# A graph kernel whose VectorE one-hots are made in pieces of three visits instead of six

## The chip, the cores and the metric

The kernel runs on one core of a Trainium2 chip. The time is the device time of one execution in microseconds (us). The kernel before was timed three times; its median is 4103.68 us. A profile is one further execution.

## The reference

The inputs are a table x of 12500 nodes by 128 features, 400000 edges (src, dst), sorted by dst, and small weights. Three times, a layer needs for every node the sum of a table's rows over its incoming edges:

```python
h = jnp.maximum(_layernorm(x, axis=-1), 0.0)
m_j = norm[:, None] * (x_j + x_j * x_i @ W1_w.T + W1_b)
out = jax.ops.segment_sum(m_j, to_, num_segments=n)       # layer 0, then a leaky relu, + x
...
agg = jax.ops.segment_sum(h[src], dst, num_segments=n)    # layers 1 and 2
mean_neigh = agg / jnp.maximum(deg, 1.0)[:, None]
return h @ W_self.T + mean_neigh @ W_neigh.T + b
```

The destinations are crowded: node numbers are drawn as the square of a uniform number, so low nodes have many edges and high nodes few.

## The kernel before, in words

Nodes are cut into 98 tiles of 128. The segment sum is made in two ways. For the low, crowded tiles ("dense", 50 in the first pass, then 56 and 57) a matrix of edge counts, 128 destinations by all 98 x 128 sources, is built in SBUF and TensorE multiplies it with the table kept in SBUF as three bf16 parts: `product` (L1460), 98 matmuls a tile. For the other tiles ("tail") the source rows of 128 edges at a time are gathered from HBM with an indirect DMA of GpSimd (`gather`, L1255) and summed by a matmul with a one-hot of the destinations (`subgroup`, L1373).

There are three passes over the graph. In pass 0 (about 285 to 1880 us) the counts of tile g are built while tile g-1 is multiplied; they are stored and loaded again in passes 1 (to about 3010 us) and 2, which build only 7 further tiles between their products.

A count matrix is built from visits. A visit takes 128 edges of blocks of one or two nodes: `visit` (L1431) is one matmul of a one-hot of the source's low 7 bits (128 columns, `hot_low`) with a one-hot of block and high bits (`hot_key`; 98 columns for a block of one node, 196 for a block of two). ScalarE moves the sums from PSUM to SBUF (L1051). VectorE makes the one-hots, `one_hots(f)`: up to 8 visits (blocks of one) or 6 visits (blocks of two) by one instruction for `hot_low` (L1682: 128 columns a visit, so 128x768 for six) and one for `hot_key` (L1685: 128x1176 for six). There are `HOTS = 3` buffers; before it fills one, VectorE waits for `s_visit`, the visits of three buffers ago, and `s_hot` tells TensorE that the buffer is full.

The tail goes in subgroups of 4 or 5 gathers. A ring holds `RSUBS = 5` of them. `ready` (L1710) makes a subgroup's destination one-hot on VectorE in one instruction (128x512 or 128x640) after `s_tail` has freed its place in the ring; `gather` waits for the same; `subgroup` on TensorE waits for `s_S` (the one-hot) and `s_gather` (the landings).

VectorE also does the element work of the layers, in pieces that are put between the one-hots by fixed tables: `take` (L1755 to L1775) reduces the sums of a tile from PSUM, `settle` (L1784 to L1797), `finish` (L1808, L1809) and `split_tile` (L1819 to L1822) follow. All engines run through orders written out beforehand; nothing is scheduled at run time. The visits per block, `vs`, come from the number of edges expected; a batch has `batches[k][1]` nodes a block (1 or 2). In the crowded front, to about 800 us, batches of one and short buffers are frequent; from 800 us on nearly all buffers have six visits of blocks of two.

Of the kernel before, what the change touches and what calls it, by code (L numbers as in the profile page):

```python
# [18 lines left out]
P = 128  # L19
# [19 lines left out]
HOTS = 3  # L39
# [95 lines left out]
def program(nc, x, src, dst, W1, b1, Ws0, Wn0, c0, Ws1, Wn1, c1, out, n_nodes):  # L135
# [111 lines left out]
    with ExitStack() as ctx:  # L247
# [1293 lines left out]
        def _(dve):  # L1541
# [129 lines left out]
            def one_hots(f):  # L1671

                k, b, m, j, n = hots[f]
                deep, width, visits = deepest[k], batches[k][1] * tiles, m * n
                c = b * deep + j
                at_c = slice(c, c + visits) if m == 1 or n == deep else slice(c, c + (m - 1) * deep + 1, deep)
# [5 lines left out]
                dve.tensor_tensor(hot_low[f % HOTS][:, 0:visits * P].rearrange("p (v f e) -> p v f e", v=visits, e=2),  # L1682
                                  low[:, k % 2, at_c, :].unsqueeze(2).to_broadcast([P, visits, P // 2, 2]),
                                  iota_l.rearrange("p (f e) -> p f e", e=2).unsqueeze(1).to_broadcast([P, visits, P // 2, 2]), ALU.is_equal)
                dve.tensor_tensor(hot_key[f % HOTS][:, 0:visits * width].rearrange("p (v f e) -> p v f e", v=visits, e=2),  # L1685
                                  key[:, k % 2, at_c, :].unsqueeze(2).to_broadcast([P, visits, width // 2, 2]),
                                  iota_k[:, 0:width].rearrange("p (f e) -> p f e", e=2).unsqueeze(1).to_broadcast([P, visits, width // 2, 2]),
                                  ALU.is_equal).then_inc(s_hot, 1)
# [14 lines left out]
            def ready(nth, n):  # L1703
# [211 lines left out]
```

## Time and profile before

| | |
|---|---|
| timed runs | 4092.16, 4103.68, 4107.59 us; median 4103.68 |
| profiled execution | 4083.7 us, span 4082.0 us, mean granted TensorE clock 0.989 |
| busy share of the span | TensorE 90%, GpSimd 70%, VectorE 49%, ScalarE 29% |
| chain that ended last | TensorE 40%, GpSimd 36%, issue 12%, VectorE 7%, DMA 4% |
| costliest groups | L1460 3054.3 us (15974 matmuls), L1255 2683.6 us (2643 gathers), L1431 1034.8 us (5102) |
| VectorE one-hots | L1682 881 instructions 475.6 us, L1685 881, 555.9 us, L1710 577, 261.0 us |

Matmuls are pipelined, so a TensorE near 100% is not at its peak. GpSimd's busy time is that of generating its indirect DMAs' descriptors; between two gathers stands a gap of 0.30 us, shown as issue time. An average over the whole span hides that the three passes have different limits.

### The profile page before, as it was taken

To read this page: it belongs to the slowest core of one execution; us is meant where nothing else is said; L and a number is where in the kernel's file an instruction comes from. 1 tells how busy PE (TensorE), PEld (TensorE's weight loads), DVE (VectorE), ACT (ScalarE), POOL (GpSimd) and SP (SyncE) were. 2 spreads that over 40 slices of the span, in tenths; PEclk is the share of its full clock that TensorE was granted. 3 is DMA by queue.
4 is the path that set the end of the run, shared out by engine and by line. 5 is a ranking of instruction groups with operands and counts; after the bars stand their busy time and mean duration, and the time that the engine had idled before them with its cause. 6 is when DMAs were issued, how large, how long until landed. Compare 5 with 4: busy or idle time off the path is not lost.

```text
span 4082.0 us, 67151 instructions
## 1 busy us (share of the span) xinstructions
PE 3657.9 (90%) x24852; PEld 2338.9 (57%) x24852; DVE 2011.0 (49%) x5255; ACT 1180.2 (29%) x3014; POOL 2848.1 (70%) x2859
## 2 busy tenths in 40 slices
PE   0028999999999999998999999999999999999998
PEld 0015666666666666665666665556555656666555
DVE  3579999977777777772233233232321113121211
ACT  0043466666666666661022021121200001000000
POOL 5603877777777777754777777777747777777775
PEclk9998999999999999999999999999999999999999
DMA  5171466666666666558776776766787776777775
GB/s 158 46 181 65 160 216 194 205 208 218 203 220 197 221 200 217 197 190 272 255 252 216 294 252 222 280 238 236 268 277 257 284 253 232 275 273 270 274 267 207
DMA packets 384251, 913.33 MB, mean 224 GB/s; under 512 B 74159, under 2 KB 318088, under 8 KB 363186
## 3 DMA queue, kind: packets, MB, share of 16 engines
q1 hardware_dynamic: 194385, 603.47, 40.0%
q0 software_dynamic: 132000, 274.23, 22.3%
q10 hardware_dynamic: 57536, 31.25, 2.8%
q8 instruction: 205, 3.36, 0.3%
q14 instruction: 125, 1.02, 0.1%
HBM read 664.23 MB, written 245.39 MB: 223 GB/s over the span
## 4 chain that ended last, share of the span: by engine, by line
PE 40%; POOL 36%; issue 12%; DVE 7%; DMA 4%; ACT 1%; DVEq 0%; POOLq 0%; ACTq 0%; SPq 0%
POOL arena L1255 33%; PE ps L1460 30%; PE ps L1373 5%; PE ps L1431 3%; DMA arena<-parts,arena 3%; DVE arena L1685 2%; DVE arena L1682 2%; POOL arena L1220 2%; PE ps L1408 2%; DMA arena<-in_dst 1%; DMA table<-arena 1%; PE ps L1398 0%; ACT arena L1130 0%; POOL arena L1245 0%; POOL arena L1230 0%
## 5 line engine op out<-in xcount | busy, mean ns | idle before, releaser
L1255 POOL DMA_INDIRECT arena<-parts,arena x2643 | 2683.6, 1015 | 950.1 <-issue 790.5
L1460 PE MATMUL ps<-arena 128*128 128x384 bf16 (+1 forms) x15974 | 3054.3, 327 | 19.1 <-DVEq L1759 11.2
L1460 PEld LDWEIGHTS ps<-arena 128*128 128x128 bf16 x15974 | 1544.1, 98 | 931.9 <-ACT arena L1051 21.8
L1051 ACT ACTIVATE arena<-ps 128x392 bf16<-128x392 f32 x1824 | 903.0, 497 | 1007.5 <-PE ps L1431 994.5
L1431 PE MATMUL ps<-arena 128*128 128x196 bf16 (+1 forms) x5102 | 1034.8, 238 | 103.4 <-DVE arena L1685 96.0
L1710 DVE TENSOR_TENSOR arena<-arena 128x640 bf16<-128x640 bf16 (+1 forms) x577 | 261.0, 462 | 1188.0 <-PE ps L1373 1186.9
L1431 PEld LDWEIGHTS ps<-arena 128*128 128x128 bf16 x5102 | 479.2, 101 | 321.4 <-DVE arena L1685 96.9
L1682 DVE TENSOR_TENSOR arena<-arena 128x768 bf16<-128x768 bf16 (+3 forms) x881 | 475.6, 540 | 247.3 <-PE ps L1431 242.6
L1373 PE MATMUL ps<-arena 128*128 128x384 bf16 (+1 forms) x2643 | 532.7, 330 | 63.2 <-DMA arena<-parts,arena 62.8
L1685 DVE TENSOR_TENSOR arena<-arena 128x1176 bf16<-128x1176 bf16 (+4 forms) x881 | 555.9, 631 | 0.0
L1373 PEld LDWEIGHTS ps<-arena 128*128 128x128 bf16 x2643 | 254.4, 98 | 228.0 <-issue 76.3
L1758 DVE TENSOR_REDUCE arena<-ps 128x128 f32<-128x384 f32 x294 | 163.0, 554 | 301.3 <-PE ps L1460 294.7
L1109 ACT ACTIVATE arena<-ps 128x128 f32<-128x128 f32 x196 | 54.1, 276 | 589.3 <-PE ps L1398 589.2
L1408 PE MATMUL ps<-w_t,arena 128*128 128x256 f32 x392 | 120.2, 389 | 20.7 <-issue 17.5
L1220 POOL DMA_INDIRECT arena<-in_dst,arena x98 | 98.0, 1000 | 55.5 <-issue 29.8
L1062 ACT ACTIVATE arena<-ps 128x128 bf16<-128x128 f32 x196 | 54.1, 276 | 281.7 <-DMA table<-arena 218.7
L1245 POOL DMA_INDIRECT arena<-records,first_edge x38 | 47.3, 1246 | 99.4 <-PE ps L1342 79.9
L1408 PEld LDWEIGHTS ps<-w_t,arena 128*128 128x128 f32 x392 | 61.1, 194 | 30.3 <-issue 23.6
L1063 ACT ACTIVATE arena<-ps 128x256 f32<-128x256 f32 x196 | 75.6, 386 | 0.0
L1819 DVE TENSOR_TENSOR arena<-arena,bias 128x128 f32<-128x128 f32 x196 | 56.1, 286 | 33.0 <-ACT arena L1063 32.6
L1323 PE MATMUL ps<-ident,arena 128*63 128x128 f32 x1 | 0.5, 475 | 71.5 <-DVE arena L1600 71.5
L1822 DVE TENSOR_TENSOR arena<-arena 128x128 bf16<-128x128 f32 x196 | 57.4, 293 | 6.8
(155 smaller groups left out, 1177.3 us busy)
## 6 DMA issues: line engine op xcount, KB each, us to landing
arena<-counts SPq DMA_DIRECT2D x102, 3136.0 KB
counts<-arena SPq DMA_DIRECT2D x56, 3136.0 KB
arena<-parts,arena POOLq DMA_INDIRECT x2643
arena<-parts SPq DMA_DIRECT2D x28, 672.0 KB, 9.6
arena<-table SPq DMA_DIRECT2D x196, 64.0 KB
parts<-arena ACTq DMA_DIRECT2D x109, 96.0 KB
parts<-arena SPq DMA_DIRECT2D x14, 679.0 KB, 7.1
parts<-arena SPq DMA_DIRECT2D x87, 96.0 KB
```

Source lines behind the costliest of these rows:

```text
L1051: act.activation(stage[k][:, :, a - g * P:b - g * P], ps[:, unit_bank(q), 0:(b - a) * tiles].rearrange("p (n a) -> p a n", n=b - a), ACT.C ...
L1063: act.activation(yS[:, n % 3, :], bank(7, 0, 2 * P), ACT.Copy).then_inc(s_yS, 1)
L1220: pool.indirect_dma_start(near[q % 7][:, t % HALF, :], None, dst.rearrange("(c e) -> c e", e=P), bass.IndirectOffsetOnAxis(ap=near_i[:, t: ...
L1255: pool.indirect_dma_start(ring[:, m % RSUBS * CHUNKS + c, 0:W0 if nth == 0 else W1C], None, parts_of[nth], bass.IndirectOffsetOnAxis(ap=ta ...
L1373: t = pe.matmul(bank(b, 0, w), S[:, e, :], ring[:, e, 0:w], start=first + c == 0, stop=first + c == tail_visits[subs[n][0]] - 1, skip_grou ...
L1408: pe.matmul(bank(7, 0, 2 * P), hT[:, r % 2, :], w_t[:, 2 * nth + 1:2 * nth + 3, :].rearrange("p k f -> p (k f)"), start=True, stop=True).t ...
L1431: pe.matmul(bank(unit_bank(q), c_0, c_0 + width), hot_low[f % HOTS][:, c * P:(c + 1) * P], hot_key[f % HOTS][:, c * width:(c + 1) * width] ...
L1460: m = pe.matmul(bank(b, 0, w), stage[k][:, a, :], Xp[:, a, 0:w], start=e == 0, stop=e == tiles - 1, skip_group_check=True)
L1682: dve.tensor_tensor(hot_low[f % HOTS][:, 0:visits * P].rearrange("p (v f e) -> p v f e", v=visits, e=2), low[:, k % 2, at_c, :].unsqueeze( ...
L1685: dve.tensor_tensor(hot_key[f % HOTS][:, 0:visits * width].rearrange("p (v f e) -> p v f e", v=visits, e=2), key[:, k % 2, at_c, :].unsque ...
L1710: dve.tensor_tensor(S[:, e:e + count, :].rearrange("p c (f e) -> p c f e", e=2), tail_rel[:, i, first:first + count, :].unsqueeze(2).to_br ...
L1758: then(dve.tensor_reduce(agg, bank(b, 0, PARTS * P).rearrange("p (k f) -> p f k", k=PARTS), AX.X, ALU.add))
```

## The change

Where a batch has blocks of two and a buffer has more than two visits, `one_hots` makes `hot_low` by two instructions and `hot_key` by two, each over half of the visits: six visits become three and three. Both halves of `hot_low` come first, then both of `hot_key`, and the last raises `s_hot`. Batches of one and buffers of two visits keep their instructions. `ready` always makes a tail subgroup's one-hot by two instructions: 128x640 as 128x256 and 128x384, 128x512 as two of 128x256; the second raises `s_S`. The waits before them are the same.

```diff
-                dve.tensor_tensor(hot_low[f % HOTS][:, 0:visits * P].rearrange("p (v f e) -> p v f e", v=visits, e=2),
...
+                halves_of = ((0, visits // 2), (visits // 2, visits)) if batches[k][1] == 2 and visits > 2 else ((0, visits),)
+                for lo, hi in halves_of:
+                    v, at_c = hi - lo, slice(c + lo * by, c + (hi - 1) * by + 1, by)
+                    dve.tensor_tensor(hot_low[f % HOTS][:, lo * P:hi * P].rearrange("p (v f e) -> p v f e", v=v, e=2),
...
+                for lo, hi in halves_of:
+                    v, at_c = hi - lo, slice(c + lo * by, c + (hi - 1) * by + 1, by)
+                    d = dve.tensor_tensor(hot_key[f % HOTS][:, lo * width:hi * width].rearrange("p (v f e) -> p v f e", v=v, e=2),
...
+                                          ALU.is_equal)
+                d.then_inc(s_hot, 1)
...
+                for lo, hi in ((0, count // 2), (count // 2, count)):
+                    d = dve.tensor_tensor(S[:, e + lo:e + hi, :].rearrange("p c (f e) -> p c f e", e=2),
+                                          tail_rel[:, i, first + lo:first + hi, :].unsqueeze(2).to_broadcast([P, hi - lo, P // 2, 2]),
+                                          iota_l.rearrange("p (f e) -> p f e", e=2).unsqueeze(1).to_broadcast([P, hi - lo, P // 2, 2]), ALU.is_equal)
+                d.then_inc(s_S, 1)
```

VectorE's queue in pass 0, where buffers have six visits (L1665 and L1667 prepare a batch's keys, L1784 begins a `settle`), before:

```order
L1682 TENSOR_TENSOR arena<-arena 128x768 [waits s_visit]
L1685 TENSOR_TENSOR arena<-arena 128x1176
L1665 TENSOR_SCALAR arena<-iota_w 128x128 [waits s_hot,s_key]
L1667 TENSOR_TENSOR arena<-ps,arena 128x256 [waits s_recps,s_ownA]
L1710 TENSOR_TENSOR arena<-arena 128x640 [waits s_tail]
L1784 SCALAR_TENSOR_TENSOR arena<-bias,s0b,ps 128x128 [waits s_w1]
```

and the same place after the change, where L1684 is the `hot_low`, L1689 the `hot_key` and L1716 the tail's one-hot:

```order
L1684 TENSOR_TENSOR arena<-arena 128x384 [waits s_visit]
L1684 TENSOR_TENSOR arena<-arena 128x384
L1689 TENSOR_TENSOR arena<-arena 128x588 x2
L1665 TENSOR_SCALAR arena<-iota_w 128x128 [waits s_hot,s_key]
L1667 TENSOR_TENSOR arena<-ps,arena 128x256 [waits s_recps,s_ownA]
L1716 TENSOR_TENSOR arena<-arena 128x256 [waits s_tail]
L1716 TENSOR_TENSOR arena<-arena 128x384
L1791 SCALAR_TENSOR_TENSOR arena<-bias,s0b,ps 128x128 [waits s_w1]
```

Three instructions have become six, and nothing has changed places. The same queue in the front of pass 0, where blocks of one have buffers of eight visits, before:

```order
L1682 TENSOR_TENSOR arena<-arena 128x1024 [waits s_visit]
L1685 TENSOR_TENSOR arena<-arena 128x784
L1710 TENSOR_TENSOR arena<-arena 128x640 [waits s_tail] x2
L1808 RECIPROCAL tile_rstd<-tile_std 128x1 [waits s_h,s_std]
L1809 SCALAR_TENSOR_TENSOR tile_shift<-tile_mv,tile_rstd 128x1 [waits s_chain]
```

and after:

```order
L1684 TENSOR_TENSOR arena<-arena 128x1024 [waits s_visit]
L1689 TENSOR_TENSOR arena<-arena 128x784
L1716 TENSOR_TENSOR arena<-arena 128x256 [waits s_tail]
L1716 TENSOR_TENSOR arena<-arena 128x384
L1815 RECIPROCAL tile_rstd<-tile_std 128x1 [waits s_h,s_std]
L1816 SCALAR_TENSOR_TENSOR tile_shift<-tile_mv,tile_rstd 128x1 [waits s_chain]
```

There only the tail's one-hots are split (the second of the two subgroups, and a buffer pair between, repeat the rows shown and are left out). The queues of the other engines are the same before and after.

## Rows read from the trace of the kernel before

**Rows 1.** Stretches: length, then busy us (count) of PE, PEld, DVE, ACT, POOL; clock, DMA, GB/s.

```profile
400.00:600.00 200.00, 188.25 (x1658) 128.16 (x1657) 189.09 (x516) 111.42 (x275) 160.99 (x129) 0.99 0.54 181
...
800.00:1812.00 1012.00, 954.38 (x6784) 657.32 (x6783) 781.25 (x2066) 629.01 (x1542) 781.59 (x731) 0.97 0.63 210
1882.00:3010.00 1128.00, 1107.16 (x6886) 677.24 (x6885) 339.55 (x889) 193.97 (x577) 819.83 (x843) 1.00 0.71 252
```

**Rows 2.** Chain of waits by line, of 400 to 600, 800 to 1812, 3010 to 4082 us.

```profile
by line: POOL arena L1255 19.9%; DVE arena L1685 19.5%; PE ps L1460 18.2%; DVE arena L1682 15.3%; PE ps L1431 7.7%; issue 7.1%; PE ps L1373 3.5%; DVE arena L1710 2.3%; DVE arena L1758 1.7%; DVE arena L1769 0.6%; POOL arena L1245 0.5%; PE ps
...
by line: POOL arena L1255 49.6%; PE ps L1460 17.1%; issue 14.6%; DMA arena<-parts,arena 5.8%; PE ps L1431 5.4%; PE ps L1373 3.8%; PE ps L1408 1.0%; POOL arena L1245 0.7%; PE ps L1386 0.4%; DVE arena L1685 0.4%; DVE arena L1682 0.3%; PE ps L
...
by line: POOL arena L1255 64.7%; issue 20.8%; PE ps L1460 8.9%; DMA arena<-parts,arena 2.8%; PE ps L1373 1.5%; DMA table<-arena 0.2%; PE ps L1408 0.1%; DVE arena L1758 0.1%; DVE arena L1773 0.1%; DVE arena L1775 0.1%; ACTq L1076 0.0%; DVE a
```

**Rows 3.** Gathers, same stretches: count | busy us, mean ns | idle before, releaser.

```profile
L1255 POOL DMA_INDIRECT arena<-parts,arena x124 | 157.3, 1269 | 37.8 <-issue 37.2 <-PE ps L1373 0.6
...
L1255 POOL DMA_INDIRECT arena<-parts,arena x713 | 762.4, 1069 | 217.3 <-issue 212.7 <-PE ps L1373 4.6
...
L1255 POOL DMA_INDIRECT arena<-parts,arena x818 | 782.1, 956 | 291.0 <-issue 248.0 <-DMA table<-arena 42.2 <-PE ps L1373 0.9
```

**Rows 4.** Timeline near 1303 us (start, us, engine), one-hots and gathers.

```profile
1301.62 0.56 DVE L1682 TENSOR_TENSOR arena<-arena 128x768 bf16<-128x768 bf16 x1 [0.97 <-PE ps L1431]
1302.09 0.77 DVE L1685 TENSOR_TENSOR arena<-arena 128x1176 bf16<-128x1176 bf16 x1
1302.77 0.55 DVE L1682 TENSOR_TENSOR arena<-arena 128x768 bf16<-128x768 bf16 x1
1303.24 0.77 DVE L1685 TENSOR_TENSOR arena<-arena 128x1176 bf16<-128x1176 bf16 x1
...
1301.77 1.23 POOL L1255 DMA_INDIRECT arena<-parts,arena  x1 [0.31 <-issue]
1303.30 1.53 POOL L1255 DMA_INDIRECT arena<-parts,arena  x1 [0.30 <-issue]
...
1306.65 0.94 POOL L1255 DMA_INDIRECT arena<-parts,arena  x1 [0.30 <-issue]
```

**Rows 5.** VectorE by form, 800 to 1812 us; then 400 to 600 us, last L1710.

```profile
L1685 DVE TENSOR_TENSOR arena<-arena 128x1176 bf16<-128x1176 bf16 x366 | 281.2, 768 | 0.0
L1682 DVE TENSOR_TENSOR arena<-arena 128x768 bf16<-128x768 bf16 x366 | 202.4, 553 | 176.4 <-PE ps L1431 174.0
L1710 DVE TENSOR_TENSOR arena<-arena 128x640 bf16<-128x640 bf16 x94 | 45.4, 484 | 0.0
...
L1710 DVE TENSOR_TENSOR arena<-arena 128x512 bf16<-128x512 bf16 x62 | 25.4, 419 | 0.0
...
L1685 DVE TENSOR_TENSOR arena<-arena 128x392 bf16<-128x392 bf16 x74 | 26.6, 359 | 0.0
...
L1685 DVE TENSOR_TENSOR arena<-arena 128x1176 bf16<-128x1176 bf16 x27 | 20.7, 765 | 0.0
...
400.00:600.00 200.00, 12.83 (x29) 0.99 0.54 181
```

**Rows 6.** Waits (total us, times, longest): 800 to 1812 us, then 400 to 600.

```profile
PE ps L1373 <- DMA arena<-parts,arena: 48.0, 13, 5.4
...
PE ps L1431 <- DVE arena L1685: 6.2, 11, 1.8
...
DVE arena L1682 <- PE ps L1431: 4.8, 14, 0.6
```

**Rows 7.** Timeline at 460 to 462 us, gathers and one-hots.

```profile
460.04 1.11 POOL L1255 DMA_INDIRECT arena<-parts,arena  x1 [0.30 <-issue]
461.45 6.75 POOL L1255 DMA_INDIRECT arena<-parts,arena  x1 [0.30 <-issue]
...
461.40 0.35 DVE L1685 TENSOR_TENSOR arena<-arena 128x392 bf16<-128x392 bf16 x1
461.67 0.28 DVE L1682 TENSOR_TENSOR arena<-arena 128x256 bf16<-128x256 bf16 x1
```

More of the change, by code:

```diff
@@ L1674, in one_hots @@
                 deep, width, visits = deepest[k], batches[k][1] * tiles, m * n
-                c = b * deep + j
-                at_c = slice(c, c + visits) if m == 1 or n == deep else slice(c, c + (m - 1) * deep + 1, deep)
+                c, by = b * deep + j, 1 if m == 1 or n == deep else deep
                 if hots[f - 1][0] != k or f == 0:
@@ L1681, in one_hots @@
                     dve.wait_ge(s_visit, hots_to[f - HOTS])
-                dve.tensor_tensor(hot_low[f % HOTS][:, 0:visits * P].rearrange("p (v f e) -> p v f e", v=visits, e=2),
[L1683 to L1688, printed above, removed]
+                halves_of = ((0, visits // 2), (visits // 2, visits)) if batches[k][1] == 2 and visits > 2 else ((0, visits),)
+                for lo, hi in halves_of:
+                    v, at_c = hi - lo, slice(c + lo * by, c + (hi - 1) * by + 1, by)
+                    dve.tensor_tensor(hot_low[f % HOTS][:, lo * P:hi * P].rearrange("p (v f e) -> p v f e", v=v, e=2),
+                                      low[:, k % 2, at_c, :].unsqueeze(2).to_broadcast([P, v, P // 2, 2]),
+                                      iota_l.rearrange("p (f e) -> p f e", e=2).unsqueeze(1).to_broadcast([P, v, P // 2, 2]), ALU.is_equal)
+                for lo, hi in halves_of:
+                    v, at_c = hi - lo, slice(c + lo * by, c + (hi - 1) * by + 1, by)
+                    d = dve.tensor_tensor(hot_key[f % HOTS][:, lo * width:hi * width].rearrange("p (v f e) -> p v f e", v=v, e=2),
+                                          key[:, k % 2, at_c, :].unsqueeze(2).to_broadcast([P, v, width // 2, 2]),
+                                          iota_k[:, 0:width].rearrange("p (f e) -> p f e", e=2).unsqueeze(1).to_broadcast([P, v, width // 2, 2]),
+                                          ALU.is_equal)
+                d.then_inc(s_hot, 1)
             def split_table(n):
@@ L1709, in ready @@
                     dve.wait_ge(s_tail, m - RSUBS + 1)
-                dve.tensor_tensor(S[:, e:e + count, :].rearrange("p c (f e) -> p c f e", e=2),
-                                  tail_rel[:, i, first:first + count, :].unsqueeze(2).to_broadcast([P, count, P // 2, 2]),
-                                  iota_l.rearrange("p (f e) -> p f e", e=2).unsqueeze(1).to_broadcast([P, count, P // 2, 2]), ALU.is_equal).then_inc(s_S, 1)
+                for lo, hi in ((0, count // 2), (count // 2, count)):
[3 more added lines that the diff above has]
+                d.then_inc(s_S, 1)
             def tail_columns(part):
```

## The prediction, made before the changed kernel was run

> **What bounds the kernel now.** I read the page's busy shares first, then the stretches [rows 1], the chain of waits cut to three of them [rows 2], the gather groups [rows 3], single gathers beside VectorE's instructions [rows 4], VectorE's shapes [rows 5] and the waits [rows 6]. The reader is to see three passes with different limits. Around 400 to 600 us VectorE is full (189 of 200 us) and GpSimd nearly (161 us, with a 0.30 us issue gap before each gather). From 800 to 1812 us TensorE is busy 954 of 1012 us, yet half of the chain is GpSimd's gather line L1255 and 14.6% is issue time, nearly all of it the gap between gathers [rows 2]. GpSimd never stands still there: 713 gathers take 762.4 us and 217.3 us of gaps, the 18 of L1245 the rest, and none waits for the ring. TensorE in turn waits 48.0 us, in 13 places, for a gather to land [rows 6]. So pass 0 runs at GpSimd's pace, with TensorE close behind. Pass 1 (1882 to 3010 us) is TensorE's: 1107 of 1128 us busy [rows 1]. In pass 2 the chain is 64.7% L1255 again.
>
> A gather costs 0.94 us when nothing is in its way (the one at 1306.65), 1.069 in the mean of 800 to 1812 us, 0.956 in pass 2 [rows 3, 4]. The single rows say why. The gather at 1303.30 began 0.06 us after a 128x1176 one-hot and took 1.53 us, 0.59 more than 0.94; the one-hot ended at 1304.01. The gather at 1301.77 took 1.23: 0.29 more, and the 128x768 one-hot before it ended at 1302.18. In both, gather start + 0.12 + the extra is the end of the VectorE instruction then running: a gather needs something once, 0.12 us after its start, that VectorE's bf16 one-hot holds until it ends. In the second case the next one-hot (1302.09) followed at once, and the gather still got through between the two. That is what halved pieces can use.
>
> **What the change does to GpSimd.** Of the shapes in rows 5, 1176 columns take 768 ns and 392 take 359: 0.52 ns a column and 0.154 us fixed. The part that holds the gather up is then 0.61 us (1176), 0.40 (768), 0.33 (640), 0.27 (512); 0.61 also fits the longest extra of rows 4, 0.59. A hold h catches a gather with chance h/T and keeps it h/2, so one instruction adds h*h/2T per gather. Over 800 to 1812 us: 366 x (0.186 + 0.080) + 94 x 0.054 + 62 x 0.036 = 104.8, by 1012 us: 0.104 us per gather; measured 1.069 - 0.94 = 0.129. In halves (588, 384, 256+384, 256+256): 366 x 0.133 + 94 x 0.029 + 62 x 0.018 = 52.5, so 0.052. The saving is 0.052 per gather by the formula, 0.065 if scaled to what was measured: 37 to 46 us over 713 gathers. I take 40.
> In 400 to 600 us only 27 hot pairs and 29 tail one-hots are split: (27 x 0.133 + 29 x 0.026)/200 x 124 gathers = 2.7 us; with the next 200 us, which are alike, 5. In pass 2 the extra is 0.016 x 818 = 13 us; half of it at best; I take 4 (0 to 7). In pass 1 nothing, since TensorE sets the pace. Sum: 49 us off GpSimd.
>
> **What it adds to VectorE.** 2 instructions for each 6-visit pair, 1 for each tail one-hot. Back to back the fixed part is mostly overlapped: 1301.62 to 1302.09 is 0.47 us for 768 columns (0.40), 1302.09 to 1302.77 is 0.68 for 1176 (0.61): 0.07 to 0.08 per added instruction; alone it is 0.154. I take 0.075, since the halves stand back to back, and keep 0.154 as the end of the range. From 800 to 1812 us that is (732 + 156) x 0.075 = 67 us. VectorE idles 174.0 us there before L1682, waiting for TensorE to release a buffer; up to 48 of it falls in TensorE's own waits for gathers, so 126 are cover and 59 stay. TensorE is up to three buffers behind VectorE, which hides most of a burst, not all: with 4.8 us of such idle time in 200 us (400 to 600) TensorE waited 6.2 us for one-hots [rows 6], which over 1012 us would be 31. The cover left, 59 us in 1012, is 2.4 times as thick, so I take about a third of 31: 11 us over the pass (0 to 31).
> From 400 to 600 us there is no cover: (54 + 29) x 0.075 = 6.2 us onto a full engine, of which the chain gives VectorE 37%. With the next 200 us I take 5 (2 to 12). The order of all other work stays; the semaphores are raised after the last piece, so a buffer is ready 0.15 us later, with two more behind it.
> What goes late next: TensorE. Its 48 us of waits are the most that pass 0 can give back after 800 us; 40 of them gone leaves 8 as margin, so VectorE's delays beyond that count in full.
> The Trainium skill, "VectorE: DVE Perf Modes", on the TRN2 errata, speaks against the change: a fixed cost per instruction with SBUF operands that shows between instructions, best spread over 512 elements or more, where the new pieces have 256 to 588. Its table's 58 cycles at 0.96 GHz would make 888 x 0.060 = 53 us (an estimate by that page), its measured 150 cycles 139 us. The rows, 0.07 to 0.08 back to back, lie near the first.
>
> **The sum.** -49 + 5 + 11 = -33 us, against the profiled execution's 4083.7 us (span 4082.0): 4051. The median of the three timed runs, 4103.7, lies 20 us above that execution, so the forecast in the median's terms is 4071.
>
> **Rivals.**
> 1. Starved gathers, slower. Between short one-hots a gather does not always get in: the one at 461.45 began on a 128x392 (461.40 to 461.75), with 128x256 and 128x392 in turn behind it, and took 6.75 us, 5.8 too much: some 20 such instructions went ahead of it [rows 7]; the same form at 460.04 took 1.11. The 400 to 600 mean, 1.269, holds such cases. The new 384-column pieces (0.20 us of hold) are as short as that 392. For it: size and back-to-back placing. Against: the 512- and 640-column tail one-hots between long ones leave the mean at 1.069, and from 800 us on VectorE pauses before a pair for 0.48 us in the mean (176.4/366), which ends a run. Price: 384-column pieces hold 366 x 2 x 0.20/1012 = 14% of the time, 103 gathers; if 4 in 10 starve (one of the two in rows 7 did) until VectorE's next pause, an estimated 1.5 us away, the length of one pair and a little, that is +62 us; with -33: +29, so 4133. It decides from about 20 starved gathers (30 us) on. Milder forms end within 0.5%.
> The Trainium skill, "SBUF — State Buffer", on the two sides of SBUF, calls the shared VectorE/GpSimd port pair an exclusive lock, the loser waiting for the instruction's end; by that alone 461.45 would have cost 0.2 extra, which row 460.04 fits and 461.45 does not.
> 2. VectorE becomes the bound. At 0.154 per instruction 888 of them are 137 us, over the 126 of cover, and TensorE waits for one-hots at the rate of 400 to 600 us (3%, 30 us), while the front loses 15 to 20. Then 49 - 30 - 18 = 1 us gained: 4103. For it: the skill's page; against: the 0.47 us step.
> 3. The holds join: a gather waits for both pieces, nothing is gained and the front loses 5 to 10 us: 4110. Against it: the gather at 1301.77 passed between two.
>
> **How the numbers follow.** Forecast 0.58, starved 0.20 (of it 0.17 slower), VectorE-bound 0.16, joined 0.06. About 0.5% (20 us) can be told from no change. The forecast's own range is -20 to -46 with some 8 us of scatter in a median (the runs shown span 15): 4050 to 4084. The wider range takes in rival 2 and the milder half of rival 1: 4050 to 4118. Faster: 0.57; within 0.5%: 0.22, rival 2, half of 3 and the weak end of the forecast; slower: 0.21.
>
> **What would show it.** Right: L1255 (same line number) at 1.00 to 1.02 us from 800 to 1812 us, the longest there near 1.25 instead of 1.53; TensorE's wait for landings down from 48.0 to under 15; the added VectorE instructions at a step of about 0.27 (384) and 0.38 (588); VectorE's wait for TensorE down from 174.0 to 60 to 90; pass 1 unchanged. Wrong: gathers of 2 us or more after 800 us (rival 1), TensorE waiting over 20 us for one-hots there (rival 2), the mean gather still 1.05 or more (rivals 1 and 3).

## The result, and the profile after

| | before | after |
|---|---|---|
| timed runs, median | 4105.64 us (4 runs, 4092.16 to 4117.82) | 4048.57 us (4 runs, 4043.56 to 4065.86) |
| ratio of the times, 95% interval | | 0.987 (0.9834 to 0.9907) |
| profiled execution, span | 4083.7, 4082.0 us | 4050.84, 4049.1 us |

The change makes the kernel faster by 1.3%. Between the two profiled executions the difference is 32.9 us, between the medians 57 us. The ratios in this document are not quotients of the two medians (here 0.986), and they leave out five slow executions of 4.9 to 10.7 ms, which fell in e2, e3, e9, e12 and before on the third chip.

The first thing to find is where it arises. The first gather of pass 1, in the timelines of GpSimd before and then after (start, us, engine; in brackets the idle time in front):

```profile
1881.77 0.94 POOL L1255 DMA_INDIRECT arena<-parts,arena  x1 [77.69 <-DMA table<-arena]
```

```profile
1848.02 0.95 POOL L1255 DMA_INDIRECT arena<-parts,arena  x1 [74.31 <-DMA table<-arena]
```

Pass 0 ends 33.8 us sooner. The first gather of pass 2, before and after:

```profile
3026.23 0.96 POOL L1255 DMA_INDIRECT arena<-parts,arena  x1 [42.16 <-DMA table<-arena]
```

```profile
2995.20 0.96 POOL L1255 DMA_INDIRECT arena<-parts,arena  x1 [41.93 <-DMA table<-arena]
```

The lead is then 31.0 us, and 32.9 at the end: pass 1 gives 2.7 us back, pass 2 adds 1.9. All of the gain is made in pass 0. There the gathers are shorter. After, by stretch (285 to 600, 600 to 800, 800 to 1770, 2995 to 4049 us), the answer to [rows 3]:

```profile
L1255 POOL DMA_INDIRECT arena<-parts,arena x135 | 170.9, 1266 | 47.5 <-issue 39.9 <-PE ps L1373 7.6
...
L1255 POOL DMA_INDIRECT arena<-parts,arena x133 | 146.9, 1104 | 40.5 <-issue 39.5 <-PE ps L1373 0.9
...
L1255 POOL DMA_INDIRECT arena<-parts,arena x718 | 730.4, 1017 | 219.0 <-issue 216.2 <-PE ps L1373 2.7
...
L1255 POOL DMA_INDIRECT arena<-parts,arena x818 | 780.2, 954 | 291.0 <-issue 247.9 <-DMA table<-arena 41.9 <-PE ps L1373 1.2
```

Before, in the first three of these stretches:

```profile
L1255 POOL DMA_INDIRECT arena<-parts,arena x139 | 177.0, 1274 | 42.4 <-issue 41.8 <-PE ps L1373 0.6
...
L1255 POOL DMA_INDIRECT arena<-parts,arena x134 | 145.8, 1088 | 40.7 <-issue 39.5 <-PE ps L1373 1.2
...
L1255 POOL DMA_INDIRECT arena<-parts,arena x690 | 738.2, 1070 | 210.3 <-issue 205.7 <-PE ps L1373 4.6
```

From 800 us on a gather takes 1017 ns instead of 1070, and 28 more of them fit into the same 970 us. In the crowded front nothing is gained, and five fewer have begun by 800 us (268 against 273). Starved gathers as in [rows 7] are still there, between two-visit buffers, which the change leaves as they were, and one is new: the gather at 403.83, where no gather of before took over 1.57 us until 441. After (the second and third row are VectorE's last pieces before the first gather got through, and what follows them):

```profile
403.83 7.13 POOL L1255 DMA_INDIRECT arena<-parts,arena  x1 [0.30 <-issue]
...
409.31 0.83 DVE L1689 TENSOR_TENSOR arena<-arena 128x588 bf16<-128x588 bf16 x2
410.06 0.15 DVE L1762 TENSOR_REDUCE s<-ps 128x1 f32<-128x3 f32 x1
...
467.46 6.81 POOL L1255 DMA_INDIRECT arena<-parts,arena  x1 [0.30 <-issue]
```

An unhindered gather takes 0.95 us, of which 0.12 lie before it asks and 0.83 behind; so this one asked at 403.95 and got through at 410.13, at the end of the last 588-column piece (409.31 + 0.83). It waited past the ends of 17 pieces that followed each other at once: one of 384 columns of the tail, two pairs of 1024 and 784 from blocks of one, and three rounds of the new 384, 384, 588, 588.

Why the gathers from 800 us on are shorter is seen in single rows, as in [rows 4]. After, near 1301 and 1307 us; "x2" are two instructions drawn as one row:

```profile
1300.90 0.59 DVE L1684 TENSOR_TENSOR arena<-arena 128x384 bf16<-128x384 bf16 x2
1301.37 0.95 POOL L1255 DMA_INDIRECT arena<-parts,arena  x1 [0.30 <-issue]
1301.41 0.83 DVE L1689 TENSOR_TENSOR arena<-arena 128x588 bf16<-128x588 bf16 x2
1302.16 0.62 DVE L1684 TENSOR_TENSOR arena<-arena 128x384 bf16<-128x384 bf16 x2
...
1307.49 0.63 DVE L1684 TENSOR_TENSOR arena<-arena 128x384 bf16<-128x384 bf16 x2 [0.29 <-PE ps L1431]
1307.67 1.01 POOL L1255 DMA_INDIRECT arena<-parts,arena  x1 [0.30 <-issue]
```

The gather at 1307.67 met the first of two 384-column pieces (1307.49 + 0.352 = 1307.84) and lost 0.06 us: it got through at 1307.85, before the second (to 1308.12). The one at 1301.37 passed between the 384s and the 588s. From 1300.90 to 1302.16, one round of four pieces, are 1.26 us, where the two instructions of [rows 4] took 1.15: an added instruction costs 0.055 us there. Over all rounds from 800 to 1770 us that have no pause, the median is 1.287 us (56 rounds) against 1.156 before (47), so 0.066 us. VectorE after, 800 to 1770 us (count | busy us, mean ns | idle before), the answer to [rows 5]:

```profile
L1689 DVE TENSOR_TENSOR arena<-arena 128x588 bf16<-128x588 bf16 x734 | 305.7, 457 | 0.0
L1684 DVE TENSOR_TENSOR arena<-arena 128x384 bf16<-128x384 bf16 x733 | 228.2, 352 | 80.4 <-PE ps L1431 77.0
L1716 DVE TENSOR_TENSOR arena<-arena 128x256 bf16<-128x256 bf16 x219 | 54.8, 285 | 0.0
```

VectorE's wait for TensorE in front of a pair, 168.2 us in this stretch before, is down to 77.0. The waits of that stretch after (total us, times, longest), against [rows 6]:

```profile
PE ps L1373 <- DMA arena<-parts,arena: 13.7, 4, 5.2
PE ps L1460 <- DVEq L1766: 9.8, 12, 1.3
...
POOL arena L1255 <- PE ps L1373: 2.7, 9, 0.3
...
PE ps L1431 <- DVE arena L1689: 1.0, 2, 0.5
```

and two of the same before:

```profile
PE ps L1373 <- DMA arena<-parts,arena: 43.7, 12, 5.4
...
PE ps L1460 <- DVEq L1759: 5.1, 8, 1.0
```

TensorE waits for landings in 4 places instead of 12, for VectorE about 5 us more, and GpSimd still hardly waits for the ring (2.7 us): busy time and gaps fill the stretch. The chain of waits after, 400 to 600 us and 800 to 1812 us, as in [rows 2]:

```profile
by line: PE ps L1460 21.7%; DVE arena L1689 20.6%; DVE arena L1684 16.8%; PE ps L1431 9.0%; POOL arena L1255 7.9%; PE ps L1373 5.1%; DMA arena<-parts,arena 4.9%; issue 3.8%; DVE arena L1716 2.9%; DVE arena L1765 1.2%; PE ps L1386 0.6%; ACT 
...
by line: PE ps L1460 42.7%; POOL arena L1255 15.9%; PE ps L1431 13.4%; PE ps L1373 7.9%; issue 5.5%; DMA arena<-parts,arena 3.9%; PE ps L1408 2.5%; DVE arena L1689 1.9%; DVE arena L1684 1.4%; PE ps L1386 1.2%; PE ps L1418 0.6%; PE ps L1398 
```

L1255 had 49.6% of the second and now has 15.9%, and TensorE's L1460 took its place. Two engines are nearly matched there now, since TensorE is busy 977 of the 1012 us; so a further gain on GpSimd alone should be cut short, though no run tests that.

The clock plays along. The stretch table before, around TensorE's longest wait for a landing (columns as in [rows 1]):

```profile
1325.00:1337.00 12.00, 12.00 (x91) 8.52 (x90) 10.30 (x28) 8.85 (x23) 9.26 (x10) 1.00 0.74 271
1338.00:1343.00 5.00, 0.20 (x1) 0.14 (x2) 0.72 (x3) 0.00 (x0) 3.78 (x5) 0.69 0.79 257
1343.00:1346.00 3.00, 3.00 (x12) 1.67 (x11) 1.22 (x3) 0.50 (x1) 2.39 (x3) 0.50 0.34 91
1346.00:1350.00 4.00, 4.00 (x28) 2.69 (x26) 2.41 (x9) 2.17 (x6) 3.09 (x4) 0.91 0.43 120
```

TensorE was fully busy at the upper level (2.4 GHz), stood still for 5.4 us, and the next 3 us of matmuls ran at 0.50, the 1.2 GHz level: 12 matmuls in 3 us, 28 in the 4 us behind. So such a wait costs TensorE more than its length. The stretches of [rows 1] after:

```profile
400.00:600.00 200.00, 184.87 (x1631) 124.62 (x1631) 189.53 (x583) 108.29 (x265) 155.53 (x126) 1.00 0.52 172
...
800.00:1812.00 1012.00, 977.20 (x7046) 676.24 (x7045) 872.91 (x3072) 651.30 (x1604) 749.55 (x736) 0.99 0.66 216
```

With a third of the waits for landings, the mean granted clock of the second is 0.99 instead of 0.97; VectorE is busy 872.91 us of it instead of 781.25.

### The profile page after: what moved, and what is told of

Its sections match the earlier page's. It is cut to its first block, busy times and chain, and to the rows that moved or that the text cites. A ratio compares the mean times of both kernels' runs of the same rounds, so it can differ in the third digit from the quotient of the medians.

```text
span 4049.1 us, 68700 instructions
## 1 busy us (share of the span) xinstructions
PE 3645.4 (90%) x24852; PEld 2332.4 (58%) x24852; DVE 2117.9 (52%) x6804; ACT 1180.1 (29%) x3014; POOL 2797.5 (69%) x2859
## 4 chain that ended last, share of the span: by engine, by line
PE 59%; POOL 20%; DVE 9%; issue 7%; DMA 4%; ACT 0%; DVEq 0%; POOLq 0%; ACTq 0%; SPq 0%
PE ps L1460 44%; POOL arena L1255 17%; PE ps L1373 7%; PE ps L1431 5%; DVE arena L1689 3%; DVE arena L1684 3%; DMA arena<-parts,arena 2%; POOL arena L1220 2%; PE ps L1408 2%; DMA arena<-in_dst 1%; DMA table<-arena 0%; PE ps L1398 0%; DVE arena L1765 0%; PE ps L1386 0%; DMA arena<-counts 0%
## 5 line engine op out<-in xcount | busy, mean ns | idle before, releaser
L1255 POOL DMA_INDIRECT arena<-parts,arena x2643 | 2635.2, 997 | 965.6 <-issue 789.5
L1460 PE MATMUL ps<-arena 128*128 128x384 bf16 (+1 forms) x15974 | 3046.3, 327 | 25.6 <-DVEq L1766 14.7
L1460 PEld LDWEIGHTS ps<-arena 128*128 128x128 bf16 x15974 | 1542.2, 98 | 934.6 <-ACT arena L1051 27.4
L1431 PE MATMUL ps<-arena 128*128 128x196 bf16 (+1 forms) x5102 | 1031.6, 238 | 110.8 <-DVE arena L1689 100.1
L1716 DVE TENSOR_TENSOR arena<-arena 128x256 bf16<-128x256 bf16 (+1 forms) x1154 | 302.2, 308 | 1171.3 <-PE ps L1373 1169.9
L1431 PEld LDWEIGHTS ps<-arena 128*128 128x128 bf16 x5102 | 477.9, 100 | 329.4 <-DVE arena L1689 101.7
L1689 DVE TENSOR_TENSOR arena<-arena 128x588 bf16<-128x588 bf16 (+4 forms) x1367 | 585.9, 458 | 0.0
L1684 DVE TENSOR_TENSOR arena<-arena 128x384 bf16<-128x384 bf16 (+5 forms) x1367 | 507.7, 400 | 135.6 <-PE ps L1431 130.5
L1373 PE MATMUL ps<-arena 128*128 128x384 bf16 (+1 forms) x2643 | 528.6, 328 | 28.3 <-DMA arena<-parts,arena 28.2
L1373 PEld LDWEIGHTS ps<-arena 128*128 128x128 bf16 x2643 | 254.3, 98 | 189.0 <-issue 35.2
L1109 ACT ACTIVATE arena<-ps 128x128 f32<-128x128 f32 x196 | 54.1, 276 | 600.5 <-PE ps L1398 597.7
L1062 ACT ACTIVATE arena<-ps 128x128 bf16<-128x128 f32 x196 | 54.1, 276 | 273.4 <-DMA table<-arena 209.6
L1408 PEld LDWEIGHTS ps<-w_t,arena 128*128 128x128 f32 x392 | 60.6, 193 | 31.9 <-issue 25.6
L1826 DVE TENSOR_TENSOR arena<-arena,bias 128x128 f32<-128x128 f32 x196 | 56.3, 287 | 32.9 <-ACT arena L1063 32.6
```

Of the source, the lines that this page charges most:

```text
L1255: pool.indirect_dma_start(ring[:, m % RSUBS * CHUNKS + c, 0:W0 if nth == 0 else W1C], None, parts_of[nth], bass.IndirectOffsetOnAxis(ap=ta ...
L1373: t = pe.matmul(bank(b, 0, w), S[:, e, :], ring[:, e, 0:w], start=first + c == 0, stop=first + c == tail_visits[subs[n][0]] - 1, skip_grou ...
L1408: pe.matmul(bank(7, 0, 2 * P), hT[:, r % 2, :], w_t[:, 2 * nth + 1:2 * nth + 3, :].rearrange("p k f -> p (k f)"), start=True, stop=True).t ...
L1431: pe.matmul(bank(unit_bank(q), c_0, c_0 + width), hot_low[f % HOTS][:, c * P:(c + 1) * P], hot_key[f % HOTS][:, c * width:(c + 1) * width] ...
L1460: m = pe.matmul(bank(b, 0, w), stage[k][:, a, :], Xp[:, a, 0:w], start=e == 0, stop=e == tiles - 1, skip_group_check=True)
L1684: dve.tensor_tensor(hot_low[f % HOTS][:, lo * P:hi * P].rearrange("p (v f e) -> p v f e", v=v, e=2), low[:, k % 2, at_c, :].unsqueeze(2).t ...
```

## The experiments

e1 to e10 differ from before only in how VectorE's one-hots are cut (e5 not at all). "Gather" is L1255's mean from 800 to 1770 us, in brackets its count there; "landings" TensorE's wait for them at L1373, "late VectorE" its wait at L1460 for VectorE, "cover" VectorE's wait for TensorE in front of a pair, all in that stretch. The profiled executions of before and after stand on top.

| | ratio (95%) | median us | gather ns | landings | late VectorE | cover |
|---|---|---|---|---|---|---|
| before | 1 | 4105.64 | 1070 (690) | 43.7 | 5.1 | 168.2 |
| after | 0.987 (0.9834 to 0.9907) | 4048.57 | 1017 (718) | 13.7 | 9.8 | 77.0 |
| e1 sliver | 0.9927 (0.9912 to 0.9942) | 4076.74 | 1051 (700) | 28.5 | 9.4 | 98.4 |
| e2 hots only | 0.984 (0.9825 to 0.9854) | 4040.28 | 1004 (716) | 9.7 | 8.8 | 80.8 |
| e3 tail only | 1.0001 (0.9991 to 1.0012) | 4107.38 | 1081 (684) | 52.7 | 5.2 | 160.5 |
| e4 uneven | 0.9906 (0.9888 to 0.9924) | 4066.45 | 1029 (712) | 21.7 | 9.4 | 84.1 |
| e5 before again | | 4097.31 | 1072 (688) | 53.6 | 5.1 | 174.9 |
| e6 key only | 0.9889 (0.9869 to 0.9909) | 4044.82 | 1015 (715) | 16.4 | 7.8 | 115.0 |
| e7 thirds | 1.0019 (1.0005 to 1.0033) | 4099.27 | 1064 (692) | 25.4 | 20.4 | 68.7 |
| e8 two slivers | 0.9969 (0.9957 to 0.9981) | 4078.11 | 1048 (702) | 19.0 | 21.7 | 53.7 |

Each ratio is against runs of before on the same chip: e1 to e4 against a median of 4105.36 us (17 runs), e6 to e8 against 4088.61 us (23 runs). e5 has a single execution.

**e1: the added instructions without the shorter pieces.** The long one-hots lose their last 2 columns of each visit to a second instruction of 12 columns; the tail's lose theirs likewise.

```diff
-                for lo, hi in halves_of:
+                for lo, hi in ((0, P // 2 - 1), (P // 2 - 1, P // 2)) if two else ((0, P // 2),):
```

> As many VectorE instructions as after the change, in the same places, but hardly shorter holds: each six-visit one-hot is made whole but for the last two columns of each visit, which a second instruction makes, and the tail's one-hots likewise. Theory (a gather waits for the rest of the VectorE one-hot that is running, so lengths count by their squares): mean gather from 800 us on 1.06 to 1.08 us as before, TensorE's waits for landings there near 48 us, time the same as before or up to 20 us longer. Rival (more gaps between VectorE instructions are what lets gathers in, whatever the lengths): mean gather near 1.02, time as after the change, some 1.3% less than before.

It was faster by 0.73%, with a gather of 1051 ns, where 1.06 to 1.08 us and no gain were expected. That is a miss for my account: as many instructions as after, nearly the old lengths, and still a third of the gathers' gain (19 of 53 ns). A hold of h catching gathers that arrive at random, h*h/2T, has no place for it. The arrivals are not random. Before, 417 to 421 us, where pair follows pair:

```profile
417.13 0.76 DVE L1685 TENSOR_TENSOR arena<-arena 128x1176 bf16<-128x1176 bf16 x1
417.18 1.52 POOL L1255 DMA_INDIRECT arena<-parts,arena  x1 [0.30 <-issue]
...
418.96 0.55 DVE L1682 TENSOR_TENSOR arena<-arena 128x768 bf16<-128x768 bf16 x1
419.01 1.32 POOL L1255 DMA_INDIRECT arena<-parts,arena  x1 [0.31 <-issue]
...
420.63 1.53 POOL L1255 DMA_INDIRECT arena<-parts,arena  x1 [0.30 <-issue]
```

VectorE's pair has a period of 1.15 us. Three gathers in a row are caught at the same two phases of it, just behind the start of an 1176 or a 768, where the hold is longest. An unhindered gather with its gap has 1.25 us; the pair with its two slivers or in halves has about 1.3. The traces from 800 to 1770 us show that e1's gathers meet the long pieces as often but later in them: behind an 1176 of before 153 gathers waited 0.355 us in the mean (half of the hold, for gathers at random, is 0.307), behind a 1164 of e1 170 waited 0.227. That the longer round is what moves them is argued, not shown.

**e2 and e3: the two parts of the change apart.** e2 halves only `hot_low` and `hot_key`, e3 only the tail's one-hots.

```diff
-                for lo, hi in ((0, count // 2), (count // 2, count)):
+                for lo, hi in ((0, count),):
```

> Only the six-visit one-hots in halves, the tail's in one piece. Theory: of the sum of squared holds, 97 of 105 are the hots', so nearly the whole gain stays: mean gather from 800 us on 1.02 to 1.03, time 35 to 55 us under before, ratio 0.987 to 0.991. Rival (the tail's one-hot matters, since it stands alone between waits): ratio over 0.995.

> Only the tail's one-hots in two pieces, the hots whole. Theory: the holds lose 3.5 of 105 units, mean gather 1.06 to 1.07, TensorE's waits for landings near 45 us, time within 5 us of before. Rival (run-to-run luck in the front gives the 20 us that the profiled executions do not show): the same small difference, but a ratio under 0.995.

e2 was faster by 1.6%, with the shortest gather of all, and beat its expectation in both (1.02 to 1.03 us, ratio 0.987 to 0.991); e3 changed nothing in the time, and its gather grew to 1081 ns, where 1.06 to 1.07 us was expected, and to 1373 ns from 285 to 600 us:

```profile
L1255 POOL DMA_INDIRECT arena<-parts,arena x129 | 177.2, 1373 | 39.3 <-issue 39.0 <-PE ps L1373 0.3
```

The tail half of the change hinders the gathers. One of the longest gathers of after shows how:

```profile
1278.72 0.46 DVE L1689 TENSOR_TENSOR arena<-arena 128x588 bf16<-128x588 bf16 x1
1279.09 0.96 DVE L1716 TENSOR_TENSOR arena<-arena 128x256 bf16<-128x256 bf16 x4
1279.55 1.32 POOL L1255 DMA_INDIRECT arena<-parts,arena  x1 [0.30 <-issue]
```

The row with "x4" names the form of its first piece alone: a one-hot of 512 columns and one of 640 stand together there, cut into 256, 256, 256 and 384. The gather's extra over 0.95 is 0.37 us. It asked at 1279.67 and got through at 1280.04, when the run of four ended (1280.05): not after the third, which it met, but after the fourth. The seven gathers of after that take over 1.3 us from 800 to 1770 us are all of this kind.

In time, e2's lead over after is not settled: their intervals overlap.

**e4: pieces of 5 visits and 1.** The same number of instructions as after, cut unevenly (640 and 128, 980 and 196; the tail's 4 or 3 subtiles and 1).

```diff
-                halves_of = ((0, visits // 2), (visits // 2, visits)) if batches[k][1] == 2 and visits > 2 else ((0, visits),)
+                halves_of = ((0, visits - 1), (visits - 1, visits)) if batches[k][1] == 2 and visits > 2 else ((0, visits),)
```

> The same number of instructions as after the change, but split 5 and 1 visits instead of 3 and 3 (tail 4 and 1 or 3 and 1). Theory of squares: (25+1)/36 = 0.72 of the holds' effect instead of 0.50, so 0.56 of the gain: mean gather from 800 us on about 1.04, time 18 to 32 us under before, ratio about 0.993. Rival (number of gaps): as after, 1.02 and 0.987. Rival (only the longest piece counts, linearly): 5/6, a third of the gain, 1.05 and 0.996.

0.9906, with 1029 ns (the squares had 0.993 and 1.04 us, a mere number of gaps 0.987 and 1.02): between e1 and after in both. At one number of instructions, the shorter the longest piece (1164, 980, 588 columns), the shorter the gather (1051, 1029, 1017 ns) and the time. Length of the hold matters beyond the rhythm.

**e5: before once more**, one profiled execution on the second chip.

> The kernel before, profiled once more: its first profiled execution took 4083.7 us, its timed runs 4105 in the median. If the difference is chance in which gathers meet which one-hots, this execution is near 4105, with the mean gather of pass 0 some 0.02 us longer than in the first profile (700 gathers, 14 us) or longer single gathers in the front; if the profiler itself makes it faster, it is again near 4084.

4097.31 us; gather 1072 ns, landings 53.6 us. The gather's mean repeats within 2 ns, the landings within 10 us and the span within 14 us: the effect on the gather in e1 to e4 is far outside that, the difference of one pair of profiles is not.

**e6: only the 1176-column one-hot halved.**

```diff
-                for lo, hi in halves_of:
+                for lo, hi in ((0, visits),):
```

(for `hot_low`; the tail's stay whole).

> Only the longest one-hot, the 128x1176, in halves; low and tail whole: one added instruction per pair instead of two. Squares: (0.093 + 0.080)/0.266 = 0.65 of the hots' effect instead of 0.50. Rhythm: a pair back to back takes 1.23 us, just under the 1.25 us from one gather's access to the next, so gathers behind each other should meet short remainders. Theory (squares plus rhythm): mean gather from 800 us on 1.01 to 1.03, time within 10 us of hots-only's 4040. Rival (squares alone): 1.03 to 1.04, time near 4065.

0.9889 and 1015 ns, with one added instruction a pair. From before, halving the longest one gives 55 ns; halving `hot_low` too gives the 11 ns to e2. The formula, scaled to the measured 0.129 us, puts 42 ns on the first and 18 on the second.

**e7: pieces of two visits** (256 and 392 columns), the tail whole.

```diff
-                halves_of = ((0, visits // 2), (visits // 2, visits)) if batches[k][1] == 2 and visits > 2 else ((0, visits),)
+                halves_of = tuple((lo, min(lo + 2, visits)) for lo in range(0, visits, 2)) if batches[k][1] == 2 and visits > 2 else ((0, visits),)
```

> The hots in pieces of two visits, six instructions per pair instead of four, tail whole. Squares: a third of the hots' effect, mean gather 1.00 or less. Rhythm: a pair then takes 1.45 us back to back, so gathers drift through the pieces and the mean stays at 1.00 to 1.01, no better than with halves. VectorE: some 1460 more instructions of 0.072 us from 800 us on, 105 us of about 120 in cover, so TensorE waits for one-hots or for L1765's reduces 10 to 30 us more: time 4045 to 4075, slower than hots-only. Rival 1 of the prediction (pieces this short starve gathers): single gathers over 2 us after 800 us and a time over 4080.

The gain is gone: 1.0019. The median gather is 0.95 us, but 36 of the 724 from 800 to 1812 us take over 1.57 us, 48 us too much together, the longest 4.65. One of them, in e7's timeline:

```profile
835.13 4.17 POOL L1255 DMA_INDIRECT arena<-parts,arena  x1 [0.30 <-issue]
835.14 0.49 DVE L1716 TENSOR_TENSOR arena<-arena 128x640 bf16<-128x640 bf16 x1
...
835.54 0.69 DVE L1684 TENSOR_TENSOR arena<-arena 128x256 bf16<-128x256 bf16 x3
...
836.15 0.90 DVE L1689 TENSOR_TENSOR arena<-arena 128x392 bf16<-128x392 bf16 x3
...
836.97 0.69 DVE L1684 TENSOR_TENSOR arena<-arena 128x256 bf16<-128x256 bf16 x3
837.58 0.90 DVE L1689 TENSOR_TENSOR arena<-arena 128x392 bf16<-128x392 bf16 x3
839.51 0.69 DVE L1684 TENSOR_TENSOR arena<-arena 128x256 bf16<-128x256 bf16 x3
```

A free gather ends 0.83 us after it got through, so this one, ending at 839.30, got through at 838.47: the end of VectorE's run of one-hots (837.58 + 0.90), after the 640 and twelve 256- and 392-column pieces. That is rival 1's starvation. The front has a worse case still:

```profile
418.32 29.08 POOL L1255 DMA_INDIRECT arena<-parts,arena  x1 [0.30 <-issue]
```

It waited past 118 VectorE instructions, all but one of them pieces of 256 or 392 columns, and 15 gathers fewer than before have begun by 800 us (258 against 273). The expected time (4045 to 4075 us) was missed; the rival held. Width alone does not say which pieces starve a gather. From 800 to 1770 us all 106 gathers of after that a 384-column piece held, with another piece at once behind it, got through at its end; of the 100 of e7 that a 392-column piece held, with another 392 behind it, 74 did, though pieces of 384 and of 392 follow each other at the same 0.27 us.

**e8: two slivers a one-hot**, which makes VectorE's round longer still at the same hold.

```diff
-                for lo, hi in ((0, P // 2 - 1), (P // 2 - 1, P // 2)) if two else ((0, P // 2),):
+                for lo, hi in ((0, P // 2 - 2), (P // 2 - 2, P // 2 - 1), (P // 2 - 1, P // 2)) if two else ((0, P // 2),):
```

(against e1; `hot_key` likewise)

> Whole one-hots again, but two slivers behind each instead of one (the last two and the two columns before them of each visit): holds as before, a pair back to back takes 1.45 us instead of 1.16 (before) and 1.30 (one sliver). Rhythm theory: from one gather's access to the next is 1.25 us; at 1.30 the next access meets the last 0.05 us of a hold, at 1.45 the last 0.20, at 1.16 it meets the start of one. So the mean gather is longer than with one sliver (1.051), 1.055 to 1.07, and the time 4080 to 4110. Rival (any slack between holds helps, the more the better): mean under 1.045 and a time under 4070.

The gather (1048 ns) is e1's; the round's length beyond 1.3 us (its median is 1.431 here) leaves the mean as it was, so the finer rule of rhythm, by which it should have grown, fell. Its ratio is worse than e1's (0.9969 against 0.9927), though on another chip and with nearly the same median, so that a loss of time against e1 is not settled. What the waits of 800 to 1770 us do show is one wait traded for another:

```profile
DVE arena L1683 <- PE ps L1431: 53.7, 65, 5.0
...
PE ps L1460 <- DVEq L1764: 21.7, 32, 1.5
```

With 53.7 us of cover left, TensorE waits 21.7 us for VectorE's reductions out of PSUM, which stand behind the one-hots, hardly at all for the one-hots (2.4 us), and 19.0 us for landings (e1: 9.4 and 28.5).

**e9 to e12** fell on a chip on which the same programs take 20% longer: before had a median of 4903.63 us there (29 runs). e9 is after, e10 is e2. e11 is e2 and e12 is before with one batch of the crowded front cut otherwise, so that most of its two-visit buffers become six-visit ones:

```diff
-        for count in ((8, 28, 32, 60) if a == 0 else (P // 2, P // 2) if vs[0] * P > 384 else (P,)):
+        for count in ((8, 28, 32, 60) if a == 0 else (64, 64) if (a, n) == (2 * P, 2) else (P // 2, P // 2) if vs[0] * P > 384 else (P,)):
```

> The changed kernel once more, beside the same with the tail's one-hots whole, on one chip. Splitting the tail costs 156 instructions of 0.07 us from 800 us on and gave a mean gather of 1.017 instead of 1.004 before. Theory: this one is 5 to 12 us slower than its neighbour with whole tails, ratio against before 0.985 to 0.989. Rival (the two differed by the chip and by chance): within 3 us of each other.

> Six-visit one-hots in halves, tail whole, beside the changed kernel. Theory: 5 to 12 us faster than it. Rival: no difference.

> Halved hots, whole tails, and in tiles 2 and 3 the 74 buffers of two visits are gathered into mostly six-visit ones (the batch is cut in two at tile 3, so its second half has two visits everywhere), which takes 50 pairs of the short 128x256 and 128x392 instructions away. Theory (runs of pieces that short starve gathers, 18 to 27 us of GpSimd's time in the front; VectorE is the bound there and loses some 60 fixed parts of 0.07 us): no gather over 2 us in 430 to 490 us, mean gather of 285 to 600 us under 1.2 instead of 1.28, time 5 to 20 us under hots-only, since TensorE's other work now bounds most of pass 0. Rival (starvation there costs nothing, since TensorE makes it up): same time as hots-only.

> The kernel before with only the front's two-visit buffers joined to six-visit ones, all one-hots whole. Pass 0 runs at GpSimd's pace here, so what the starved gathers cost should come back in full: theory 10 to 20 us under before, ratio 0.995 to 0.9975. Rival (the gathers would then meet longer one-hots instead and gain nothing): ratio 0.998 to 1.002.

| | median us | ratio (95%) | gather ns, 960 to 2120 us | gather ns, 340 to 720 us |
|---|---|---|---|---|
| e9 after | 4947.09 | 1.0101 (1.0063 to 1.0138) | 1002 | 1149 |
| e10 hots only | 4925.0 | 1.0052 (1.003 to 1.0075) | 998 | 1163 |
| e11 hots only, front joined | 4929.41 | 1.006 (1.0039 to 1.0081) | 997 | 1045 |
| e12 before, front joined | 4890.47 | 0.9983 (0.9952 to 1.0015) | 1044 | 1150 |

Here the change is a loss of 1.0%, where a gain of 1.1 to 1.5% was expected, though the gathers are shorter (1002 ns against e12's 1044; before itself has no profile from there, e12 is the nearest). e9, 960 to 2120 us, GpSimd's and then TensorE's group:

```profile
L1255 POOL DMA_INDIRECT arena<-parts,arena x644 | 645.0, 1002 | 494.5 <-PE ps L1373 264.3 <-issue 167.3 <-remote 62.8
...
L1431 PE MATMUL ps<-arena 128*128 128x196 bf16 x2016 | 499.6, 257 | 196.5 <-issue 100.2 <-ACT arena L1051 95.0 <-DVE arena L1689 0.5
```

and e12's:

```profile
L1255 POOL DMA_INDIRECT arena<-parts,arena x657 | 686.2, 1044 | 453.1 <-PE ps L1373 230.2 <-issue 174.8 <-remote 48.1
```

GpSimd waits 264.3 us for TensorE to free its ring, where it waited 2.7 us from 800 to 1770 us in the profile of after shown above. It does not set the pace, so shorter gathers have nothing to give (its waits are 230.2 us with e12's 1044 ns and 239.1 to 264.3 with the 997 to 1002 of e9 to e11), and TensorE never waits for a landing in that stretch. TensorE in turn stands 100.2 us in "issue", time for which the profile shows no cause, but e12 has more of that (130.7). What e9 to e11 have more of than e12 is TensorE's wait at L1431 for ScalarE, which empties PSUM: 95.0, 78.1 and 97.3 us against 54.1. Pass 0 ends 40.5 us later in e9 than in e12, but e10 and e11, which differ in the front alone, also lie 26 us apart there, so one pair of profiles does not place the loss. Why that chip is slower was not tried and stays open, and so does why the shorter pieces cost time there: VectorE still has 254.9 us of waits for TensorE, and TensorE only 15.1 us for VectorE at L1460.

In e11 the joined front shortens its gathers from e10's 1163 to 1045 ns, and none is over 1.57 us there. e12 has 1150, near e9's 1149; before itself, its proper measure, has no profile on that chip, so that a joined front helps only where what replaces the two-visit pieces is cut in halves is a guess. The time of e11 stays at e10's (their intervals overlap), and e12's at before's, where 10 to 20 us less was expected. What the starved front costs on the first two chips stays open.

## Why the prediction was right, and where not

The mechanism and the sign were right, and the sum of -33 us is what the spans differ by, 32.9. That it meets them so closely is luck, since its terms were not all of that size. The median, 4048.57 us, is 22 us below the 4071 forecast and 1.4 below the lower end of the range, 4050; only as a ratio (0.987 of 4103.68 is 4050.3) does it lie just inside. Of the signs named, the mean gather (1.017 us), the waits for landings (13.7 us), the cover (78.9 us from 800 to 1812) and the steps (0.27 and 0.375 us) came as said; the longest gather was 1.32 instead of 1.25. The terms:

- **GpSimd from 800 us on (-40).** 713 gathers x (1069 - 1017 ns) = 37 us. Checked on the end of the gathers: the idle time before pass 1 began at 1881.77 - 77.69 = 1804.1 before and at 1848.02 - 74.31 = 1773.7 after, 30.4 us sooner, which is 37 less the five gathers (5 x 1.3 us = 7) by which after was behind at 800 us. The rest of the 33.8 us is the shorter stretch behind the last gather (3.4 us).
- **The front (-5 and +5).** The -5 failed: gathers there are as long as before (1274 to 1266, 1088 to 1104 ns), and after is some 7 us behind at 800 us, where the two terms made 0. Six gathers over 1.57 us stand from 400 to 600 us, together 25.6 us over 0.95 each; before and e5 have four, 18.4 us. Five more, of 1.6 to 2.1 us, stand from 600 to 800 us in after and none in before, e2 or e6, whose tail is whole. And GpSimd waits once, at 452.38, 6.67 us for TensorE to free the ring; e1, e2, e4, e6 and e8 have such a wait of 4.4 to 6.8 us, before, e5, e3 and e7 have none over 1 us. Why it arises was not followed up. e5, the same kernel as before, was 3 gathers behind it, so that part of the 7 us can be scatter.
- **VectorE's bursts (+11).** This step failed in size: the cover left was 77.0 us, as estimated (60 to 90), but TensorE's added waits for VectorE are 0.8 us at L1431 and 4.7 us at L1460. They delayed no gather from 800 us on (GpSimd's waits for TensorE went from 4.6 to 2.7 us), and while GpSimd sets the pace a wait of TensorE's that reaches no gather is free. The term came out near 0. It was taken from 400 to 600 us, where TensorE waits at another place; what really comes late first is L1460 behind L1766, as e7 and e8 show with 68.7 and 53.7 us of cover.
- **Passes 1 and 2 (0 and -4).** +2.7 and -1.9 us; pass 2's gathers went from 956 to 954 ns.

So 37 + 3 + 2 = 42 us were saved instead of 49, and 7 + 3 = 10 paid instead of 16: two errors that cancel. The formula behind the -40 was not right either: it lets gathers arrive at random, and e1, with hardly shorter holds, has a third of their gain.

**The tail** was counted on the wrong side. The prediction's formula gave its split 94 x 0.025 + 62 x 0.018 = 3.5 of the 52.3 by which its sum fell, a gain of 2 to 3 us; e3 shows the gather 11 ns longer, and e2 without the split 13 ns shorter than after, 9 us over 718 gathers, where the spans of e2 and after differ by 11. On the third chip e10 is 22 us under e9, though their intervals overlap.

**The step from the execution to the median (+20).** It assumed that after's median would lie above its profiled execution as before's did. Before's profiled execution was among its fastest (4083.7 against 4092.16 to 4117.82), after's was not (4050.84, median 4048.57). Runs of before scatter by 24 us on one chip (4081.16 to 4105.13), and its pass 1 alone differs by 8 us between two profiles (1144.5 and 1152.4 us, e5). The gain of 57 us in the medians is therefore more than the 33 that the profiles explain; e2 and e6 gained 65 and 44 against the medians of before on their chips. e1 shows the same gap: 29 us in the medians, 2.2 between its profiled span (4079.8) and before's. What makes up the difference was not found.

**Rival 1** (starved gathers) was right as a mechanism and too dark on how often 384 and 588 columns cause it: none from 800 us on in after (the longest gather is 1.32 us), one in e2 (2.06 us at 807.95, held past a 588 and two whole 640s), one in the front of after (7.13 us at 403.83), against 36 with 256 and 392 (e7). In e7 it would have "decided from about 20", and 48 us of delay from 800 us on with 48 more from 400 to 600 us (before 18) ate the whole gain. The Trainium skill, "SBUF — State Buffer", on the two sides of SBUF, has VectorE or GpSimd wait for the end of the other's one instruction; by that alone the gather of e7 at 835.13 would have been through at 835.6, and it was at 838.47. The measurement decides.

**Rival 2** (VectorE the bound) did not come in after, since an added instruction costs 0.055 to 0.066 us and not 0.154. The fixed cost in the Trainium skill, "VectorE: DVE Perf Modes", on the TRN2 errata, 58 cycles or 0.060 us, lies between these two; its advice to tile by 512 elements or more would have kept the whole pieces, and 384 columns (e2 against e6) gained 11 ns a gather.

**Rival 3** (the holds join) fell for the hots from 800 us on: gathers pass between 384s and 588s. It can come true in runs with 256-column pieces, and at 403.83 it did for 384s and 588s too.

## What to carry to other kernels

Where GpSimd's indirect DMAs set the pace, look for the VectorE instruction that each long one runs into, and cut the longest of these first: halving the 1176 alone gave most of the gain. Stop above 256 to 392 columns, and don't place short pieces in a closed run, since a gather can then wait for the run's end. Look for single gathers of several us afterwards, in every stretch: the mean hides them, and 384 and 588 columns are not safe in themselves (403.83). Ask first whether GpSimd really sets the pace: with the ring's wait at 264 us instead of 3, the same cut costs 0.5 to 1.0%. The best version on the chips where the cut gains is e2, with the tail's one-hots whole, by its gather and its median, though its interval overlaps that of after.

## What the runs showed that was not expected

- Long one-hots that follow each other at 1.15 us hold successive gathers at the same phase (1.52, 1.32, 1.53 us at 417 to 421 us); adding two 12-column instructions shortened the mean gather by 19 ns.
- Between 256- and 392-column pieces a gather can wait for over a hundred instructions (29.08 us in e7), and once for twelve of 384 and 588 in a row of 17. The steps from piece to piece, 0.20 us for 256 and 0.27 for 392 (e7: (0.69 - 0.284)/2, (0.90 - 0.354)/2), 0.27 for 384 and 0.37 for 588 (after: 0.62 - 0.352, 0.83 - 0.457), don't tell why 384 lets nearly all pass and 392 does not; it stays open.
- One chip of those used ran the same program 20% slower (4903.63 us). VectorE's durations were the same there (588 columns: 458 ns, against 457), but TensorE's were not: in e9 the matmuls of L1460 were busy 3270.0 us against 3046.3 in after, at a mean granted clock of 0.944 against 0.996.
